# Feed-forward layer of a Perceiver kernel: weight blocks split three tiles ahead, output products four tiles behind, variances and powers of seven token tiles made in the layer before

## The chip, the cores and the metric

The kernel runs on one core of a Trainium2 chip. The metric is the device time of one launch in microseconds (us), the median of several runs. The engines are named as in the profile: PE is TensorE's matrix products, PEld its loads of the stationary operand (they overlap PE), DVE is VectorE, ACT is ScalarE, POOL is GpSimd, SP issues most of the DMAs. Every engine works through its own instructions in program order and waits on semaphores for the others.

## The reference, cut to what matters

Six layers follow each other on x, 16 sequences of 64 tokens with 512 features: 1024 tokens, which the kernel holds as 8 tiles of 128. The change touches the last two.

```python
x = x + _L1_attn_ref(_layernorm(x), ...)    # decayed attention: a scan over 64 steps, then y @ W_o.T
x = x + _L1_ffn_ref(_layernorm(x), ...)     # feed-forward

h = einsum('bsd,df->bsf', x, w1) + b1       # 512 -> 2048
h = float2fix(h, 8)                         # round to multiples of 1/256
h = pwlin_gelu_basic(h, 8, 8)               # 33-point piecewise linear GELU
out = einsum('bsf,fd->bsd', h, w2) + b2     # 2048 -> 512
return float2fix(out, 8)
```

A layernorm is (x - mean) / sqrt(variance + 1e-5) for each token.

## The kernel before

The layers run one after another. Between two of them all engines meet at a barrier, short blocks of semaphore instructions (L2376, L2378) come next, and then each engine starts on its own program of the next layer.

**The scan layer** (`decayed_attention_layer`) does 64 steps in NG = 8 groups of G = 8. Its output product of the last group, `out_proj(7)`, ends on PE after the last step; DVE then adds it to x in `add_out(7)` (L1956). Ahead of that addition DVE makes the statistics of token tiles 0 to 6 for the next layer: seven `bn_stats` (L2028) and seven `bn_aggr` (L2031), mean and variance into `mv6`. GpSimd's last work in this layer is long done by then.

**The feed-forward layer** (`feed_forward_layer`) works on NGR = 2 groups of TG = 4 token tiles (512 tokens), and in each on FT = 16 tiles of 128 hidden features: N = 32 tiles, numbered n. Its entry: DVE adds epsilon to four variances (`var6`, L2292), makes the statistics of token tile 7 (L2293, L2294) and adds epsilon to the other four (L2295); GpSimd raises each four to the power -1/2 (`rs6`, L2112). DVE normalises four tiles (`norm`, L2265), PE turns them (`turn`, L2149), ACT copies the rounded high part into `xT` (`norm_out`, L2170) and DVE makes the rest, the low part (`rest_x`, L2258). Group 1's four tiles go the same way between the tiles n = 1 and 11.

For every tile n:

- ACT copies a 128x128x4 block of w1 as the high part (`first_w`, L2175), DVE makes its low part (`rest_w`, L2270). The blocks lie in a ring of WR = 3.
- PE makes `hidden(n)` (L109): 12 products of 512 columns, high by high, high by low and low by high for four feature blocks, in one of three banks.
- ACT scales and adds the bias (L2181) and rounds (L2186), in `stage_a(n)`; DVE clamps (`round_(n)`, L2230 and L2234).
- ACT finds the knot and evaluates GELU at the two ends of the step, in `stage_b(n)` (L2196, L2199, L2201); GpSimd takes their difference (`slope(n)`, L2106).
- DVE interpolates in four instructions (`interpolate(n)`, L2245, L2248, L2250, L2252), into `hs`, a ring of HR = 4.
- PE makes `output(n)` (L2137): four fp32 products of 512 columns, which the trace shows as eight, added up over the 16 tiles of a group in four banks.

The program order is written by hand. On PE it is `hidden(n)` and then `output(n - LAG)` with LAG = 3, and after the last hidden tile the three outputs that are left. On ACT it is `first_w(n + 2)` (from n = 1), `stage_a(n + 1)`, `stage_b(n)`. On DVE it is `round_(n + 1)`, `rest_w(n + 2)` (from n = 1), `interpolate(n)`, then what belongs to single tiles: `norm` of a tile of group 1 behind n = 1, 3, 5, 7, `rest_x` behind n = 4, 6, 8, 10. When group 0 is complete, DVE takes its four banks (`sum_out`, L2282) behind `interpolate(17)` and finishes one tile (`finish`, L2288, L2289) behind each of n = 18 to 21. PE's `output(16)`, the first of group 1, waits for each bank to be taken; it stands behind `hidden(19)`. The end of the kernel is `sum_out` and `finish` of the four tiles of group 1 and their DMAs to DRAM.

The two order lines that matter are

```python
for n in range(N):                       # PE
    hidden(n)
    ...
    if n >= LAG:
        output(n - LAG)
```

Of the kernel before, what the change touches and what calls it, by code (L numbers as in the profile page):

```python
# [11 lines left out]
ALU = mybir.AluOpType  # L12
# [3 lines left out]
P = 128  # L16
B, S, D = 16, 64, 512
J, C = 512, 384
NT = B * S // P
# [10 lines left out]
LN_EPS = 1e-5  # L30
# [1554 lines left out]
def decayed_attention_layer(nc, a, e):  # L1585
# [9 lines left out]
    with ExitStack() as st:  # L1595
# [43 lines left out]

        e.open_sems()  # L1640
        with nc.Block() as block:
# [20 lines left out]
            @block.gpsimd  # L1662
            def _(pool):
                for c in range(NG):
                    ln.pool(pool, c)

# [203 lines left out]
            def _(ve):  # L1870
# [161 lines left out]
                ch.link(ins)  # L2032
                add_out(NG - 1)


def feed_forward_layer(nc, a, e):
# [13 lines left out]
    with ExitStack() as st:  # L2050
        def sbuf(name, shape, dt=F32):
            return st.enter_context(nc.sbuf_tensor(name, shape, dt))

        WR, HR, LAG = 3, 4, 3
# [9 lines left out]
        st6, mv6, var6, rs6 = e.st6, e.mv6, sbuf("var6", [P, NT]), sbuf("rs6", [P, NT])  # L2064
        xn = z
        var_sb, rs_sb, n_sb, n_mm = sem("var6s"), sem("rs6s"), sem("n_sb6"), sem("n_mm6")
# [19 lines left out]
        with nc.Block() as block:  # L2086
# [13 lines left out]
            def _(pool):  # L2100
# [8 lines left out]
                for g in range(NGR):  # L2109
                    now = slice(g * TG, (g + 1) * TG)  # L2110
                    pool.wait_ge(var_sb, BASE + g + 1)
                    nc.gpsimd.tensor_tensor(rs6[:, now], var6[:, now],  # L2112
                                            cn[:, CN_MHALF:CN_MHALF + 1].to_broadcast([P, TG]),
                                            ALU.pow).then_inc(rs_sb, 1)
# [51 lines left out]
            def _(act):  # L2166
# [45 lines left out]
                for n in range(N):  # L2212
                    if n and n + 2 < N:
                        first_w(n + 2)
# [7 lines left out]
            def _(ve):  # L2222
# [38 lines left out]
                def norm(t):  # L2261
                    ve.wait_ge(rs_sb, BASE + t // TG + 1)
# [29 lines left out]
                nc.vector.tensor_scalar(var6[:, 0:TG], mv6[:, 0:TG, 1], LN_EPS, None, ALU.add).then_inc(var_sb, 1)  # L2292
                ch.link(nc.vector.bn_stats(st6[:, NT - 1, :], x[:, NT - 1, :]))  # L2293
                ch.link(nc.vector.bn_aggr(mv6[:, NT - 1, :], st6[:, NT - 1, :]))  # L2294
                nc.vector.tensor_scalar(var6[:, TG:NT], mv6[:, TG:NT, 1], LN_EPS, None, ALU.add).then_inc(var_sb, 1)  # L2295
# [6 lines left out]
                rest_w(2)  # L2302
                ve.wait_ge(s_b, BASE + 32)
# [3 lines left out]
                for n in range(N):  # L2307
                    if n + 1 < N:
                        round_(n + 1)
                    if n and n + 2 < N:  # L2310
                        rest_w(n + 2)
# [15 lines left out]
def perceiver_kernel(nc, a, out):  # L2327

    ctx = ExitStack()
    with ctx:  # L2330
# [76 lines left out]
        env.mv6 = x[:, NT, 64:64 + NT * 2].rearrange("p (t s) -> p t s", t=NT)  # L2407
        env.out, env.xg_d, env.yg_d, env.x_d = out, xg_d, yg_d, x_d
# [66 lines left out]
```

## Time and profile before

| | us |
|---|---|
| median of 3 runs | 2140.75 |
| lowest and highest | 2139.08, 2141.41 |
| the profiled execution | 2137.46 |
| its span | 2135.7 |
| PE busy | 1910.4 (89%) |
| DVE busy | 1345.1 (63%) |
| ACT busy | 1137.0 (53%) |
| POOL busy | 124.1 (6%) |
| mean granted TensorE clock | 0.935 |

All times in the rows are microseconds from the start of the span, and durations unless a column says otherwise. The scan layer ends at about 1905, the feed-forward layer starts at 1906.6 and runs to the end: some 229 us of 2135.7. A clock of 1.00 is 2.4 GHz, of 0.50 it is 1.2 GHz. "[0.33 <-DVE ws L2270]" behind a row says that the engine was idle for 0.33 us ahead of it, until the named instruction released it; "<-issue" names no instruction that it waited for.

### The profile page before, as it was taken

The numbers are of one execution on the slowest core, as the hardware profiler recorded it, in microseconds if no ns is written. First come the engines' busy times: TensorE is split into PE (matmuls) and PEld (weight loads), VectorE is DVE, ScalarE is ACT, GpSimd is POOL, SyncE is SP. The second block draws the span as 40 slices with busy tenths as digits, with TensorE's granted clock in tenths as the row PEclk, the third lists the DMA queues.
The fourth block names the chain that finished last, engine by engine and source line by source line (L and its number), as shares of the span: only waits on it lengthen the run. The fifth ranks groups of instructions, "written<-read, shape, count | busy, mean of one in ns | idle before, by whom it ended". The sixth has DMA issues, their size and how long they took to land. (4 is left out here: it accounts for less than half of the span.)

```text
span 2135.7 us, 31829 instructions
## 1 busy us (share of the span) xinstructions
PE 1910.4 (89%) x10570; PEld 1511.8 (71%) x10570; DVE 1345.1 (63%) x2457; ACT 1137.0 (53%) x1878; POOL 124.1 (6%) x153
## 2 busy tenths in 40 slices
PE   7978875599999589999999999999977999888998
PEld 4647764599999467787878787878755676665654
DVE  4755663599999364545353636363527899986676
ACT  5753331588888254444453535454435666656654
POOL 0000001200000111000000000000000000001221
PEclk9998985799999799999999999999998788879999
DMA  7410004244431521100000000000204000020000
GB/s 259 158 55 1 0 0 202 87 175 152 187 142 54 202 75 60 35 30 34 29 34 29 34 29 34 29 34 29 79 28 147 1 1 1 1 84 1 0 20 20
DMA packets 25897, 137.47 MB, mean 64 GB/s; under 512 B 4066, under 2 KB 4194, under 8 KB 22116
## 3 DMA queue, kind: packets, MB, share of 16 engines
q1 hardware_dynamic: 19588, 116.18, 14.7%
q0 software_dynamic: 6240, 20.45, 2.8%
q8 instruction: 33, 0.54, 0.1%
q14 instruction: 36, 0.29, 0.0%
HBM read 116.17 MB, written 20.45 MB: 64 GB/s over the span
## 5 line engine op out<-in xcount | busy, mean ns | idle before, releaser
L109 PE MATMUL PS<-cT,qs 128*128 128x512 f32 x1152 | 295.5, 402 | 9.0 <-ACT pb L1406 7.0
L109 PE MATMUL PS<-pT,cN 128*128 128x512 f32 x1152 | 270.2, 392 | 1.7 <-DVE pT L1501 1.7
L109 PEld LDWEIGHTS PS<-cT,qs 128*128 128x128 f32 x1152 | 209.4, 189 | 59.8 <-issue 15.1
L109 PEld LDWEIGHTS PS<-pT,cN 128*128 128x128 f32 x1152 | 213.9, 188 | 45.5 <-DVE pT L1501 1.9
L109 PE MATMUL PS<-fw,xgT 128*128 128x384 f32 x1104 | 204.2, 340 | 3.1 <-DVE xgT L1049 3.0
L109 PEld LDWEIGHTS PS<-fw,xgT 128*128 128x128 f32 x1104 | 191.5, 189 | 8.4 <-issue 4.5
L1049 DVE TENSOR_TENSOR fw<-W,fw 128x1536 fp32r<-128x1536 f32 x92 | 159.3, 1753 | 44.7 <-ACT fw L972 44.7
L1496 DVE TENSOR_REDUCE nmax<-PS 128x1 f32<-128x512 f32 x128 | 87.7, 685 | 157.0 <-PE PS L109 156.9
L109 PE MATMUL PS<-ws,xT 128*128 128x512 f32 x672 | 180.6, 427 | 6.6 <-DVE ws L563 4.9
L109 PEld LDWEIGHTS PS<-ws,xT 128*128 128x128 f32 x672 | 137.6, 207 | 46.1 <-issue 11.3
L972 ACT ACTIVATE fw<-W 128x1536 fp32r x92 | 134.2, 1486 | 50.2 <-issue 50.2
L1401 ACT ACTIVATE qp<-PS 128x512 f32<-128x512 f32 x96 | 57.4, 598 | 189.8 <-PE PS L109 189.8
L1501 DVE TENSOR_TENSOR pT<-PS,pT 128x512 fp32r<-128x512 f32 x128 | 86.9, 684 | 52.6 <-ACT pT L1423 52.6
L2137 PE MATMUL PS<-W,hs 128*128 128x512 f32 x256 | 114.9, 593 | 2.9 <-DVE z L2282 1.7
L109 PE MATMUL PS<-xT,ws 128*128 128x512 f32 x384 | 103.0, 418 | 9.8 <-DVE ws L2270 8.4
L1423 ACT ACTIVATE pT<-PS 128x512 fp32r<-128x512 f32 x128 | 75.5, 597 | 65.6 <-PE PS L1301 65.4
L946 PE MATMUL PS<-pw,hT 128*128 128x512 f32 x414 | 101.8, 400 | 4.7 <-DVE hT L1049 4.7
L1406 ACT ACTIVATE pb<-PS,nmax 128x512 f32<-128x512 f32 x128 | 87.5, 684 | 34.4 <-DVE nmax L1496 34.3
L1713 PEld LDWEIGHTS PS<-cn,W 128*128 128x128 f32 x512 | 79.0, 228 | 36.9 <-DVE W L2025 30.3
L109 PEld LDWEIGHTS PS<-xT,ws 128*128 128x128 f32 x384 | 72.7, 191 | 38.7 <-DVE ws L2270 18.1
L1713 PE MATMUL PS<-cn,W 128*128 128x16 f32 x512 | 78.1, 287 | 21.9 <-DVE W L2025 21.7
L1524 DVE COPY qp<-PS 128x512 f32<-128x512 f32 x48 | 33.1, 691 | 100.0 <-PE PS L1338 100.0
(259 smaller groups left out, 3390.6 us busy)
## 6 DMA issues: line engine op xcount, KB each, us to landing
W<-in_fc SPq DMA_DIRECT2D x8, 3072.0 KB, 10.5
cT<-in_ctxT SPq DMA_DIRECT2D x16, 768.0 KB, 5.4
raw_pj<-in_proj SPq DMA_DIRECT2D x8, 1536.0 KB, 6.5
ct_in<-in_ctxT SPq DMA_DIRECT2D x16, 768.0 KB
cn_in<-in_ctxN SPq DMA_DIRECT2D x16, 768.0 KB
W<-in_w SPq DMA_DIRECT2D x2, 4096.0 KB, 12.9
routed_x<-zero SPq DMA_DIRECT2D x23, 256.0 KB, 5.4
xg<-routed_x POOLq DMA_DIRECT2D x23, 256.0 KB, 3.2
```

What stands on the lines that cost most here:

```text
L109: mm = nc.tensor.matmul(out, lhs(m, s), rhs(n, s), start=(opens and (s, m, n) == terms[0]), stop=((s, m, n) == terms[-1]))
L946: mm = nc.tensor.matmul(ps[7], hT[m][:, f, :], pw[n][:, f, :], start=(f == 0 and m == n), stop=(f == FK - 1 and m == 1))
L972: nc.scalar.activation(fw[0][:, :, fc_cols(c)], raw_fc_of(par, c), ACT.Copy).then_inc(fc_hi, 1)
L1049: return nc.vector.tensor_tensor(out, whole, first.bitcast(F32), ALU.subtract)
L1401: nc.scalar.activation(out, src, ACT.Copy, scale=scale).then_inc(w_sb, count)
L1406: nc.scalar.activation(pb[:, g % 2, :], ps[g % 2], ACT.Exp, bias=nmax[:, g % 4:g % 4 + 1], accum_out=rsum[:, g % 4:g % 4 + 1]).then_inc(e_ ...
L1423: nc.scalar.activation(turned(pT[0], g), ps[2 + g % 2].rearrange("p (j n) -> p j n", j=JK), ACT.Copy).then_inc(pt_hi, 1)
L1496: nc.vector.tensor_reduce(nmax[:, g % 4:g % 4 + 1], ps[g % 2], AX.X, ALU.max, negate=True).then_inc(m_dve, 1)
L1501: return nc.vector.tensor_tensor(out, whole, first.bitcast(F32), ALU.subtract)
L1524: nc.vector.tensor_copy(heads, src).then_inc(qp_dve, 1)
L1713: mm = nc.tensor.matmul(ps[6 + c % 2][:, col:col + B], rb[:, t % RB, k * P:(k + 1) * P], sel, start=True, stop=True)
L2137: mm = nc.tensor.matmul(ps[HB + t], hs[:, n % HR, t * P:(t + 1) * P], w26[:, f, :], start=(f == 0), stop=(f == FT - 1))
```

## The change

Four things are edited; nothing that is computed changes.

- The variances plus epsilon of token tiles 0 to 6 are made on DVE in the scan layer, between `bn_aggr` and `add_out(7)`, in one instruction, and GpSimd raises them to the power there, ahead of the barrier. `var6` and `rs6` move into a spare row of x, and two more semaphores carry the two hand-overs.
- In the feed-forward layer the first four `norm` are the first instructions of DVE. The statistics, the epsilon and the power of token tile 7 come later, behind `rest_w(2)`. Only `norm(7)` waits for GpSimd.
- Weight blocks are split one tile earlier: `first_w(n + 3)` and `rest_w(n + 3)` from n = 0, in the same ring of three.
- LAG is 4: PE makes `hidden(n)` and then `output(n - 4)`, and four outputs follow the last hidden tile. The ring of `hs` stays at four.

```diff
@@ scan layer, GpSimd, behind its last normalisation
+                pool.wait_ge(var_sb, BASE + 1)
+                nc.gpsimd.tensor_tensor(e.rs6[:, 0:NT - 1], e.var6[:, 0:NT - 1],
+                                        cn[:, CN_MHALF:CN_MHALF + 1].to_broadcast([P, NT - 1]), ALU.pow).then_inc(rs_sb, 1)
+                pool.wait_ge(rs_sb, BASE + 1)
@@ scan layer, DVE, its end
                 for t in range(NT - 1):
                     ins = nc.vector.bn_aggr(e.mv6[:, t, :], e.st6[:, t, :])
                 ch.link(ins)
+                nc.vector.tensor_scalar(e.var6[:, 0:NT - 1], e.mv6[:, 0:NT - 1, 1], LN_EPS, None,
+                                        ALU.add).then_inc(var_sb, 1)
                 add_out(NG - 1)
@@ feed-forward layer
-        WR, HR, LAG = 3, 4, 3
+        WR, HR, LAG = 3, 4, 4
...
@@ GpSimd
-                for g in range(NGR):
-                    now = slice(g * TG, (g + 1) * TG)
-                    pool.wait_ge(var_sb, BASE + g + 1)
-                    nc.gpsimd.tensor_tensor(rs6[:, now], var6[:, now],
-                                            cn[:, CN_MHALF:CN_MHALF + 1].to_broadcast([P, TG]),
-                                            ALU.pow).then_inc(rs_sb, 1)
+                pool.wait_ge(var_sb, BASE + 1)
+                nc.gpsimd.tensor_tensor(rs6[:, NT - 1:NT], var6[:, NT - 1:NT], cn[:, CN_MHALF:CN_MHALF + 1],
+                                        ALU.pow).then_inc(rs_sb, 1)
@@ ACT
-                    if n and n + 2 < N:
-                        first_w(n + 2)
+                    if n + WR < N:
+                        first_w(n + WR)
@@ DVE
                 def norm(t):
-                    ve.wait_ge(rs_sb, BASE + t // TG + 1)
+                    if t == NT - 1:
+                        ve.wait_ge(rs_sb, BASE + 1)
...
-                nc.vector.tensor_scalar(var6[:, 0:TG], mv6[:, 0:TG, 1], LN_EPS, None, ALU.add).then_inc(var_sb, 1)
-                ch.link(nc.vector.bn_stats(st6[:, NT - 1, :], x[:, NT - 1, :]))
-                ch.link(nc.vector.bn_aggr(mv6[:, NT - 1, :], st6[:, NT - 1, :]))
-                nc.vector.tensor_scalar(var6[:, TG:NT], mv6[:, TG:NT, 1], LN_EPS, None, ALU.add).then_inc(var_sb, 1)
                 for t in range(TG):
                     norm(t)
                 rest_w(0)
...
                 rest_w(1)
                 rest_w(2)
+                ch.link(nc.vector.bn_stats(st6[:, NT - 1, :], x[:, NT - 1, :]))
+                ch.link(nc.vector.bn_aggr(mv6[:, NT - 1, :], st6[:, NT - 1, :]))
+                nc.vector.tensor_scalar(var6[:, NT - 1:NT], mv6[:, NT - 1:NT, 1], LN_EPS, None,
+                                        ALU.add).then_inc(var_sb, 1)
...
                     if n + 1 < N:
                         round_(n + 1)
-                    if n and n + 2 < N:
-                        rest_w(n + 2)
+                    if n + WR < N:
+                        rest_w(n + WR)
                     interpolate(n)
```

The lines below are programs in order, one row for one kind of instruction, with its output and inputs; in the changed kernel the lines of the file stand some further down, so the same instruction has another number. First PE, from the start of the feed-forward layer: the turns of group 0 (z to PS), hidden tiles (ws by xT) and output tiles (hs by W). Before:

```order
L2149 MATMUL PS<-cn,z 128x128 x16
L109 MATMUL PS<-xT,ws 128x512 x48
L2137 MATMUL PS<-W,hs 128x512 x4
L109 MATMUL PS<-xT,ws 128x512 x12
L2137 MATMUL PS<-W,hs 128x512 x4
```

And in the changed kernel:

```order
L2153 MATMUL PS<-cn,z 128x128 x16
L109 MATMUL PS<-xT,ws 128x512 x60
L2141 MATMUL PS<-W,hs 128x512 x4
L109 MATMUL PS<-xT,ws 128x512 x12
L2153 MATMUL PS<-cn,z 128x128 x4
```

Five hidden tiles (60 products) now stand ahead of `output(0)`, where four stood.

Second DVE, from the last statistics of the scan layer to the weight block of tile 2. Before:

```order
L2031 BN_AGGR x<-x 128x2 x7
L1956 TENSOR_TENSOR x<-x,PS 128x512
L1641 UNCONDITIONAL_BRANCH
L2378 UNCONDITIONAL_BRANCH
L2376 UNCONDITIONAL_BRANCH
L2221 UNCONDITIONAL_BRANCH
L2292 TENSOR_SCALAR var<-x 128x4
L2293 BN_STATS x<-x 128x6
L2294 BN_AGGR x<-x 128x2
L2295 TENSOR_SCALAR var<-x 128x4
L2265 TENSOR_SCALAR z<-x,rs 128x512 x4
L2270 TENSOR_TENSOR ws<-W,ws 128x512
```

And in the changed kernel, where var6 and rs6 are parts of x:

```order
L2036 BN_AGGR x<-x 128x2 x7
L2038 TENSOR_SCALAR x<-x 128x7
L1961 TENSOR_TENSOR x<-x,PS 128x512
L1642 UNCONDITIONAL_BRANCH
L2383 UNCONDITIONAL_BRANCH
L2381 UNCONDITIONAL_BRANCH
L2225 UNCONDITIONAL_BRANCH
L2270 TENSOR_SCALAR z<-x 128x512 x4
L2275 TENSOR_TENSOR ws<-W,ws 128x512
L2262 TENSOR_TENSOR xT<-PS,xT 128x4x128 x4
L2275 TENSOR_TENSOR ws<-W,ws 128x512 x2
L2304 BN_STATS x<-x 128x6
```

The four small instructions have left the place ahead of the first normalisation (z); one of their kind stands ahead of the addition that ends the scan layer, three behind the third weight block.

Third DVE again, the first two tiles. Before, `round_(1)`, `interpolate(0)`, `round_(2)`, `rest_w(3)`, and the start of `interpolate(1)`:

```order
L2230 TENSOR_SCALAR c<-r 128x512
L2234 TENSOR_SCALAR up<-r 128x512
L2245 SCALAR_TENSOR_TENSOR y<-km,c 128x512
L2248 SCALAR_TENSOR_TENSOR y<-y,dg 128x512
L2250 SCALAR_TENSOR_TENSOR y<-g,y 128x512
L2252 SCALAR_TENSOR_TENSOR hs<-y,up 128x512
L2230 TENSOR_SCALAR c<-r 128x512
L2234 TENSOR_SCALAR up<-r 128x512
L2270 TENSOR_TENSOR ws<-W,ws 128x512
```

And in the changed kernel:

```order
L2234 TENSOR_SCALAR c<-r 128x512
L2238 TENSOR_SCALAR up<-r 128x512
L2275 TENSOR_TENSOR ws<-W,ws 128x512
L2249 SCALAR_TENSOR_TENSOR y<-km,c 128x512
L2252 SCALAR_TENSOR_TENSOR y<-y,dg 128x512
L2254 SCALAR_TENSOR_TENSOR y<-g,y 128x512
L2256 SCALAR_TENSOR_TENSOR hs<-y,up 128x512
L2234 TENSOR_SCALAR c<-r 128x512
L2238 TENSOR_SCALAR up<-r 128x512
L2275 TENSOR_TENSOR ws<-W,ws 128x512
```

`rest_w(3)` now stands ahead of `interpolate(0)`, and the block that stands behind `round_(2)` is that of tile 4.

## Rows read from the trace of the kernel before

**Rows 1.** The page's head: the span of the profiled execution.

```profile
span 2135.7 us, 31829 instructions
```

**Rows 2.** Windows: length, busy us and count of PE, PEld, DVE, ACT, POOL, clock.

```profile
1980.00:2034.00 54.00, 54.00 (x180) 33.18 (x179) 35.31 (x62) 34.31 (x54) 11.60 (x9) 1.00 0.00 0
```

**Rows 3.** Line L2270 (`rest_w`): who waited for it, us in total and times.

```profile
  PEld PS L109: 18.1, 25
```

**Rows 4.** Timeline of PEld in steady state: start, us, engine, line, operation.

```profile
1981.78 0.19 PEld L109 LDWEIGHTS PS<-xT,ws 128*128 128x128 f32 x1 [0.33 <-DVE ws L2270]
1982.12 2.47 PEld L109 LDWEIGHTS PS<-xT,ws 128*128 128x128 f32 x11 [0.16 <-issue]
...
1988.30 0.19 PEld L109 LDWEIGHTS PS<-xT,ws 128*128 128x128 f32 x1 [0.24 <-issue]
1988.73 2.48 PEld L109 LDWEIGHTS PS<-xT,ws 128*128 128x128 f32 x11 [0.24 <-issue]
...
2001.07 2.47 PEld L109 LDWEIGHTS PS<-xT,ws 128*128 128x128 f32 x11 [0.16 <-issue]
...
2007.24 2.47 PEld L109 LDWEIGHTS PS<-xT,ws 128*128 128x128 f32 x11 [0.16 <-issue]
```

**Rows 5.** Timeline of the entry into the feed-forward layer.

```profile
1904.54 0.69 DVE L1956 TENSOR_TENSOR x<-x,PS 128x512 f32<-128x512 f32 x1 [1.00 <-PE PS L1723]
...
1906.67 0.17 DVE L2292 TENSOR_SCALAR var<-x 128x4 f32<-128x4 f32 x1 [1.44 <-PEq L2376]
...
1906.92 2.09 POOL L2112 TENSOR_TENSOR rs<-var,cn 128x4 f32<-128x4 f32 x2 [96.25 <-DVE var L2292]
...
1907.97 1.92 DVE L2265 TENSOR_SCALAR z<-x,rs 128x512 f32<-128x512 f32 x4
...
1912.63 0.69 DVE L2258 TENSOR_TENSOR xT<-PS,xT 128x512 fp32r<-128x512 f32 x1 [0.16 <-ACT xT L2170]
...
1913.38 8.48 PE L109 MATMUL PS<-xT,ws 128*128 128x512 f32 x36 [1.41 <-DVE xT L2258]
```

**Rows 6.** Timeline of the first tiles, and PEld's fifth hidden tile.

```profile
1920.65 0.43 DVE L2230 TENSOR_SCALAR c<-r 128x512 f32<-128x512 f32 x1 [1.89 <-ACT r L2186]
...
1928.07 1.75 DVE L2270 TENSOR_TENSOR ws<-W,ws 128x512 fp32r<-128x512 f32 x1
...
1929.87 4.38 PE L109 MATMUL PS<-xT,ws 128*128 128x512 f32 x12 [8.01 <-DVE ws L2270]
...
1937.52 2.50 PEld L109 LDWEIGHTS PS<-xT,ws 128*128 128x128 f32 x11 [0.16 <-issue]
```

**Rows 7.** Windows of half a us, columns as in rows 2: where the clock changes.

```profile
1908.50:1909.00 0.50, 0.43 (x4) 0.43 (x4) 0.50 (x3) 0.00 (x0) 0.50 (x1) 0.92 0.94 360
...
1912.00:1912.50 0.50, 0.00 (x0) 0.00 (x0) 0.47 (x1) 0.50 (x2) 0.00 (x0) 0.67 0.15 66
...
1925.50:1926.00 0.50, 0.00 (x0) 0.00 (x0) 0.50 (x1) 0.50 (x2) 0.00 (x0) 0.99 0.00 0
...
1932.50:1933.00 0.50, 0.50 (x3) 0.36 (x3) 0.50 (x2) 0.00 (x0) 0.00 (x0) 0.68 0.00 0
```

**Rows 8.** Timeline at the group boundary: PEld's hidden tiles and DVE's `sum_out`.

```profile
2031.91 2.24 PEld L109 LDWEIGHTS PS<-xT,ws 128*128 128x128 f32 x10 [0.16 <-issue]
...
2035.62 2.48 DVE L2282 TENSOR_TENSOR z<-PS,b 128x512 f32<-128x512 f32 x4
...
2046.79 2.47 PEld L109 LDWEIGHTS PS<-xT,ws 128*128 128x128 f32 x11 [0.16 <-issue]
...
2071.93 2.47 PEld L109 LDWEIGHTS PS<-xT,ws 128*128 128x128 f32 x11 [0.16 <-issue]
```

**Rows 9.** Timeline of the tail: the last `hs`, and PE's last two output tiles.

```profile
2111.86 0.69 ACT L2181 ACTIVATE h<-PS,b1q 128x512 f32<-128x512 f32 x1 [2.74 <-PE PS L109]
...
2119.93 7.13 PE L2137 MATMUL PS<-W,hs 128*128 128x512 f32 x16 [1.24 <-DVE hs L2252]
...
2121.97 0.69 DVE L2252 SCALAR_TENSOR_TENSOR hs<-y,up 128x512 f32<-128x512 f32 x1
```

More of the change, by code:

```diff
@@ L1638, in now @@
             return slice(G * c, G * (c + 1))
+        var_sb, rs_sb = sem("var6s"), sem("rs6s")
         e.open_sems()
@@ L2063, in feed_forward_layer @@
         y = sbuf("y6", [P, 2, 512])
-        st6, mv6, var6, rs6 = e.st6, e.mv6, sbuf("var6", [P, NT]), sbuf("rs6", [P, NT])
+        st6, mv6, var6, rs6 = e.st6, e.mv6, e.var6, e.rs6
         xn = z
-        var_sb, rs_sb, n_sb, n_mm = sem("var6s"), sem("rs6s"), sem("n_sb6"), sem("n_mm6")
+        var_sb, rs_sb, n_sb, n_mm = sem("var7s"), sem("rs7s"), sem("n_sb6"), sem("n_mm6")
         s_b, b_q, dve = sem("s_b6"), sem("b_q6"), sem("dve6")
@@ L2407, in perceiver_kernel @@
         env.mv6 = x[:, NT, 64:64 + NT * 2].rearrange("p (t s) -> p t s", t=NT)
+        env.var6, env.rs6 = x[:, NT, 96:96 + NT], x[:, NT, 112:112 + NT]
         env.out, env.xg_d, env.yg_d, env.x_d = out, xg_d, yg_d, x_d
```

## The prediction, made before the changed kernel ran

> **What bounds the kernel now.** I read the page's head first: the span is 2135.7 us [rows 1], and the profiled execution took 2137.46, so 1.76 us lie around the span. The median is 2140.75, 3.29 above that execution; I work out a difference against the profiled execution and take it from the median. The change touches only the last 229 us, so the next view is the windows of the feed-forward layer. In steady state PE is busy for 54.00 of 54 us at clock 1.00 [rows 2]: it is the bound there, DVE has 35.31 us of work and ACT 34.31. From the start of products in one hidden tile to the next it takes 2007.24 - 2001.07 = 6.17 us [rows 4]: the loads of a hidden tile are 0.228 apart ((2.47 - 0.19) / 10), so its 12 products take 2.74 us, and the rest, 3.43, is the output tile. This work is the same after the change. What can move is the time in which PE stands still between 1906 and the end, in four places.
>
> The view of who waited for whom offers more than there is: PE's loads wait 18.1 us in all, 25 times, for `rest_w` [rows 3]. In steady state such a wait is 0.33 us, and the next load then follows after 0.16 (0.49 together); a tile without the wait has 0.24 and 0.24 (0.48) [rows 4]. The second load starts when the array takes the first product, and it comes at the same point either way: the wait lies under the last output product. The Trainium skill ("TensorE: Matmul & The Clock Gate", Part 2, step-by-step) says that the next tile's weights load while this tile's products run; by that rule the 18.1 us are not for sale, and the 0.49 against 0.48 agree.
>
> **The entry.** Before, DVE's first work is at 1906.67, and the first normalisation starts at 1907.97, behind the epsilon and GpSimd's power [rows 5]. After, the normalisation is DVE's first instruction: 1.30 us sooner. DVE carries the chain from there (four normalisations, a weight block, four low parts), idle only 0.16 us before the last low part [rows 5], which may go too; I take 1.30. What is moved out costs nothing in its new places, by these covers. In the scan layer one epsilon instruction (0.17, as at 1906.67) falls into the 1.00 us in which DVE waits for PE's last output product [rows 5]. GpSimd's power follows at about 1903.8 and takes 1.05 (2.09 for two of them) [rows 5]: it ends at about 1904.9, DVE's addition at 1905.23, so the barrier is not held up, with 0.3 us of cover; a power that takes 0.7 longer would cost 0.4. Token tile 7's statistics (about 1.1 us of DVE) come behind `rest_w(2)`, at about 1913.4, and the bias follows at 1915.1. ACT needs it for `stage_a(0)`, when `hidden(0)` is done: start 1913.38 - 1.30 = 1912.08, and the first product group takes some 3.1, so 1915.2. Cover 0.1; at worst a few tenths.
>
> **The clock at the entry** is the first thing I cannot read off. PE fell to half clock within 1908.50 to 1909.00 and rose within 1912.00 to 1912.50 [rows 7], after it had been idle from 1904.4 on: about 3.4 us at half clock, all under the turns of group 0, before products began at 1913.38. After the change the turns are over by about 1909.1, PE then waits until 1912.1 for DVE, and such a stretch may come later and lie on the products. Bounds: nothing, or 3.4 us at half clock on products, which loses 1.7. The nearest row is the stretch of [rows 7] itself, and I see no reason that it should end before 1912.1 again; I take half, 0.8 lost. The skill (same page, Part 1) says the monitor runs freely and doesn't restart with the work, so that the point of change shifts between runs; by that rule the loss would also differ between executions. The sum does without it.
>
> **The first tiles.** Before, PE finishes `hidden(2)` at about 1921.9 and stands idle for 8.01 us until `rest_w(3)` is done at 1929.8 [rows 6]. That instruction waits behind the whole `interpolate(0)`, which waits for GELU's table and for GpSimd. After, `rest_w(3)` stands behind `round_(1)`, 0.43 + 0.42 after 1920.65 - 1.30 [rows 6], so it is ready at 1920.9, and `hidden(3)` goes almost without a wait (0.3 us). Then PE stands before `hidden(4)`, for the block that is now in the old place of `rest_w(3)`: DVE and ACT do the same before it, shifted by 1.30. It starts at 1929.87 - 1.30 = 1928.6. So the stop stays (about 5 us in place of 8), but one more hidden tile is done ahead of it: 2.74 us gained. Here the clock comes in again: it fell at about 1926.0 and rose at about 1932.8 [rows 7], and the tile at 1929.87 took until 1937.52 where 6.17 and 0.22 for the first load would have made 1936.26 [rows 6]: 1.26 lost. A stop of 5 us may lose up to 1.7, or nothing, which is 0.44 less or 1.26 more than before; I take the same loss as before, since an idle time of 4.2 us at the entry already brought the fall [rows 7].
>
> Behind it DVE must keep up: `rest_w(4)` will take 1.75, as the block in this place does now next to GpSimd's difference, where 0.69 is usual [rows 6]. The skill ("GPSIMD Engine Reference", Key points) says that GpSimd shares its SBUF interfaces with a VectorE instruction of two SBUF inputs; by the rule the stretch is of this kind. I count `interpolate(1)` 2.9, `norm(4)` 0.54, `round_(3)` 0.85, `rest_w(5)` 0.69 from 1928.6: 1933.6, against `output(0)` ending at 1928.6 + 0.2 + 2.74 + 3.43 = 1935.0. One more stretch of 1.06 still fits.
>
> **The group boundary.** From product to product it takes 2046.79 - 2031.91 = 14.88 us for two tiles, where 12.34 are due: 2.54 lost [rows 8]. `sum_out` (2.48) starts at 2035.62, `output(16)` waits for it, and `hidden(20)` for the weight block behind it. The next four tiles take 2071.93 - 2046.79 = 25.14 for 24.68: 0.46 more, from the four `finish` on DVE. Together 3.00. After, `output(15)` stands behind `hidden(19)`, so `sum_out` must wait 3.43 us longer for it, with DVE idle; but `rest_w(20)` is done before that, and PE has `hidden(20)`, 2.74 us, while DVE takes the banks; the first is free after 0.7. Then `rest_w(21)` is due 2.74 + 3.43 = 6.17 after `output(15)` and ready at 2.48 + 0.85 + 0.69 = 4.0. DVE's tile with a `finish` is 0.43 + 0.42 + 0.69 + 4 x 0.69 + 1.12 = 5.4 us with some gaps, under 6.17, so it catches up. All 3.00 gained; at least 0.
>
> **The tail.** The last hidden tile's result is taken at 2111.86; its `hs` is ready at 2122.66, and PE stood idle for 1.24 for the one before it [rows 9]. After, four outputs (13.7 us) stand between `hidden(31)` and `output(31)`, more than the 10.8 that `hs(31)` needs. 1.24 gained. What follows, four times `sum_out` and `finish`, is unchanged.
>
> **The ring of hs** has four places, and LAG = 4 leaves none spare: `interpolate(n)` needs `output(n - 4)`. DVE comes to it behind `round_(n + 1)`, thus behind `hidden(n + 1)`, which stands behind `output(n - 4)` on PE. The wait is over before it is met.
>
> **Sum:** 1.30 + 2.74 + 3.00 + 1.24 = 8.28, less 0.8 for the clock at the entry: 7.5 us. 2137.46 - 7.5 = 2129.96 for the profiled execution, 2140.75 - 7.5 = 2133.2 for the median. With the clock at its best (0 and 1.26 back) 9.5, 2131.2; at its worst (1.7 and 0.44) 6.1, 2134.6.
>
> **Rivals.** (1) The stop at the boundary stays: DVE stands still longest there, since `sum_out` now waits for `output(15)`, and the work behind it might reach PE after all. For: DVE idles 2.5 us more. Against: 2.1 us of cover at `rest_w(21)`. Price 3.00; with the clock at its worst the gain is 3.1: 2137.6, within 0.2%. (2) Slower: DVE becomes the bound, by meeting GpSimd. In steady state GpSimd's difference runs while DVE waits for it; should the new order put `rest_w` and another two-input instruction of each tile next to it, each stretches from 0.69 to 1.75 [rows 6], and DVE's tile grows from 4.3 plus 0.2 of gaps to 6.6, past 6.17. It decides from 6.17 on, and costs 0.43 on 28 tiles, 12 us: 2145.2. Against it: `rest_w(n + 3)` takes the very slot of `rest_w(n + 2)`. (3) The load waits do cost array time: 18.1 more, 2115. [rows 4] speak against it. (4) The change does nothing at the entry, since GpSimd's power holds the barrier as long as it did the normalisation: 1.30 less, 2134.5, inside my case.
>
> **How the numbers follow.** My case 0.76 (2131.2 to 2134.6), rival 1 0.12, rival 2 0.06, rival 3 0.03, others 0.03. A median of three lies within about 1.7 of another (2139.08 to 2141.41), so the range is 2131.2 - 1.7 = 2129.5 up to 2137.5, into rival 1. A measurement tells about 0.2%, 4.3 us, from no change: faster 0.84, same 0.10, slower 0.06.
>
> **What would show it.** The first normalisation right behind the barrier, at 1906.7; a stop of about 5 us before the fifth hidden tile and none before the fourth; tiles of 6.17 with load gaps of 0.24; no wait of PE at the boundary and at the last outputs; the clock's half-rate stretches between 1909 and 1933. It would be wrong if DVE's low parts of weights came later than their tile, if tiles of 6.17 grew, or if the stop before `hidden(4)` were as long as the old one.

## The result, and the profile after the change

The changed kernel takes 2133.49 us in the median of 20 runs (2130.25 to 2138.08); the kernel before took 2140.01 in 20 runs beside it (2136.43 to 2144.98). The ratio is 0.9968, with a 95% interval of 0.996 to 0.9977: about 6.9 us faster by the ratio, 6.5 by the two medians. The prediction was 2133.2 and 7.5 us.

The profiled executions tell less at first sight: 2136.46 us with a span of 2134.6 after, against 2137.46 and 2135.7 [rows 1], only 1 us apart. The reason lies ahead of the layer. The last statistics of the scan layer are the same instruction in both kernels, and nothing ahead of them was changed; yet they start at 1898.69 before and at 1903.15 after. The first row below is of the kernel before, the others of the changed one (timeline: start, us, engine, line, operation, and in brackets what the engine waited for):

```profile
1898.69 4.25 DVE L2028 BATCH_NORM_STATS2 x<-x 128x6 f32<-128x512 f32 x7
```

```profile
1903.15 4.25 DVE L2033 BATCH_NORM_STATS2 x<-x 128x6 f32<-128x512 f32 x7
...
1908.04 0.17 DVE L2038 TENSOR_SCALAR x<-x 128x7 f32<-128x7 f32 x1
1908.29 1.49 POOL L1668 TENSOR_TENSOR x<-x,cn 128x7 f32<-128x7 f32 x1 [93.55 <-DVE x L2038]
...
1910.64 0.69 DVE L1961 TENSOR_TENSOR x<-x,PS 128x512 f32<-128x512 f32 x1 [2.42 <-PE PS L1728]
...
1912.76 1.92 DVE L2270 TENSOR_SCALAR z<-x 128x512 f32<-128x512 f32 x4 [1.44 <-PEq L2381]
```

So this execution came to the changed code 4.46 us late. In the 14 traces of this case the same instructions start anywhere from 1896.13 (e4 below, mean granted clock of the execution 0.937) to 1906.29 (e5, 0.929). And DVE waited 2.42 for the scan layer's last products instead of 1.00 [rows 5], since they ran at half clock and took 5.40 us, where the trace of before has 3.70 (the timeline of PE, before and after):

```profile
1900.73 3.70 PE L1723 MATMUL PS<-W,yT 128*128 128x512 f32 x8 [1.18 <-ACT yT L1811]
```

```profile
1905.20 5.40 PE L1728 MATMUL PS<-W,yT 128*128 128x512 f32 x8 [1.18 <-ACT yT L1816]
```

That isn't the change's either: the traces of e1 and e2 below, which have the old entry, show the same 5.40, as do all others; of 14 traces that of before alone has 3.70. Whoever compares the two spans puts these 6 us on the change. I compare the layer with itself: from the start of DVE's first instruction in it to the end of DVE's last. Before, 1906.67 [rows 5] to 2131.77; after, 1912.76 to 2130.80. The ends are these rows, before and after:

```profile
2131.08 0.69 DVE L2289 SCALAR_TENSOR_TENSOR x<-z,x 128x512 f32<-128x512 f32 x1
```

```profile
2130.11 0.69 DVE L2294 SCALAR_TENSOR_TENSOR x<-z,x 128x512 f32<-128x512 f32 x1
```

That is 225.10 against 218.04: **7.06 us shorter**, which agrees with the medians. Everything below is read on this measure, called the layer's time.

**The start after the change.** The timeline of PE, with the DVE instructions it waits for. It answers to [rows 5, 6]:

```profile
1918.36 8.46 PE L109 MATMUL PS<-xT,ws 128*128 128x512 f32 x36 [1.41 <-DVE xT L2262]
...
1926.29 0.68 DVE L2275 TENSOR_TENSOR ws<-W,ws 128x512 fp32r<-128x512 f32 x1
...
1927.03 3.01 PE L109 MATMUL PS<-xT,ws 128*128 128x512 f32 x12 [0.21 <-DVE ws L2275]
...
1931.78 0.69 DVE L2256 SCALAR_TENSOR_TENSOR hs<-y,up 128x512 f32<-128x512 f32 x1
...
1933.06 1.76 DVE L2275 TENSOR_TENSOR ws<-W,ws 128x512 fp32r<-128x512 f32 x1
...
1934.87 5.49 PE L109 MATMUL PS<-xT,ws 128*128 128x512 f32 x12 [4.83 <-DVE ws L2275]
...
1943.40 0.19 PEld L109 LDWEIGHTS PS<-xT,ws 128*128 128x128 f32 x1 [0.24 <-issue]
```

The stop of 8.01 us ahead of `hidden(3)` [rows 6] is gone (0.21 is left), and one of 4.83 stands ahead of `hidden(4)`. The windows show the clock there; column eight is the granted clock:

```profile
1933.50:1934.00 0.50, 0.00 (x0) 0.00 (x0) 0.50 (x1) 0.47 (x2) 0.50 (x1) 0.79 0.00 0
1934.00:1934.50 0.50, 0.00 (x0) 0.00 (x0) 0.50 (x1) 0.50 (x2) 0.27 (x1) 0.50 0.00 0
...
1940.50:1941.00 0.50, 0.50 (x2) 0.18 (x1) 0.47 (x2) 0.50 (x1) 0.00 (x0) 0.88 0.00 0
```

From its start `hidden(4)` needs until 1943.40 - 1934.87 = 8.53 us to the next hidden tile's load; 5.96 are due (a tile of 6.17 and 0.22 for the first load, less 0.43 from a first load to the second). So the clock takes 2.57 here, where it took 1.26 in the trace of before. By these windows it fell at 1933.8 and rose at 1940.6: 6.8 us at half clock, as long as the stretch from 1926.0 to 1932.8 in [rows 7].

**Steady state and boundary.** The window is again 54 of 54 us of PE at full clock, as [rows 2]; the timeline of PEld and DVE around the group boundary answers to [rows 4, 8]:

```profile
1984.00:2038.00 54.00, 54.00 (x179) 32.86 (x177) 34.87 (x60) 34.50 (x54) 10.32 (x8) 1.00 0.00 0
```

```profile
2031.60 0.19 PEld L109 LDWEIGHTS PS<-xT,ws 128*128 128x128 f32 x1 [0.24 <-issue]
...
2037.77 0.19 PEld L109 LDWEIGHTS PS<-xT,ws 128*128 128x128 f32 x1 [0.24 <-issue]
...
2038.40 2.48 DVE L2287 TENSOR_TENSOR z<-PS,b 128x512 f32<-128x512 f32 x4 [2.57 <-PE PS L2141]
...
2041.46 0.69 DVE L2275 TENSOR_TENSOR ws<-W,ws 128x512 fp32r<-128x512 f32 x1
...
2043.93 0.19 PEld L109 LDWEIGHTS PS<-xT,ws 128*128 128x128 f32 x1 [0.24 <-issue]
...
2050.10 0.19 PEld L109 LDWEIGHTS PS<-xT,ws 128*128 128x128 f32 x1 [0.24 <-issue]
```

Three tiles, 18.50 us, 6.17 each: nothing is lost at the boundary, though DVE now stands idle for 2.57 ahead of `sum_out`. It is close, though: each of the next four tiles, those with a `finish`, takes DVE 6.21 us (its `round_` starts at 2040.80, 2047.01, 2053.22, 2059.43 and 2065.64), a little more than PE's 6.17. Who waited for `rest_w` (line L2275) shrank from [rows 3] to

```profile
  PEld PS L109: 6.1, 3
```

and the tile still takes 6.17. Twelve us of load waits left the profile and brought nothing.

**The tail.** PE's 40 last output products come in one piece; before, the last 16 stood behind a wait of 1.24 [rows 9]:

```profile
2108.76 17.33 PE L2141 MATMUL PS<-W,hs 128*128 128x512 f32 x40
```

In the page's chain (section 4, shares of the span) the engines' row is now

```profile
PE 9%; DVE 0%; ACT 0%; issue 0%; POOL 0%; DVEq 0%
```

so the end hangs on PE's own work alone, back to the stop at the start.

**Where the 7.06 us are:** first products 5.60 us after DVE's first instruction instead of 6.71, 1.11; one more hidden tile ahead of the stop, 2.74; clock in the stop, -1.31; boundary, 3.00; tail, 1.52 (the wait of 1.24 and the loads behind it). Sum 7.06.

Two of these terms belong to the executions and not to the change. The -1.31 is one: e3 below has the old stop of 8.02 us and loses 2.6 behind it, and the changed kernel in a second trace (e12) loses 1.3 behind its stop of 4.82. The 1.11 is the other: on the way to the first products lie the turns, and they took 3.39 us in the trace of before and 3.58 in that of after, by where half clock fell. Where half clock covers the turns whole, the products start 6.99 us after DVE's first instruction with the old entry (e1, e2) and 5.69 with the new one (e6, e11, e12): 1.30. Without the clock the traces give 1.30 + 2.74 + 3.00 + 1.52 = 8.56. The medians give 6.5, and their interval reaches from 4.9 to 8.6. Whether more clock is lost in the changed kernel on the mean of many executions, one or two traces of each kernel can't tell.

### The profile page after: what moved, and what is told of

The parts are those of the page before. It is cut to its first block and busy times, and to the rows that moved or that the text cites. A ratio compares the mean times of both kernels' runs of the same rounds, so it can differ in the third digit from the quotient of the medians.

```text
span 2134.6 us, 31828 instructions
## 1 busy us (share of the span) xinstructions
PE 1920.8 (90%) x10570; PEld 1522.1 (71%) x10570; DVE 1352.5 (63%) x2457; ACT 1137.2 (53%) x1878; POOL 125.5 (6%) x153
```

## The experiments

Theory A works as the prediction does, place by place along PE's order, but it was written behind the result and knows more: in e1, e2 and e4 it says that the lag of four costs at the start, which the prediction does not. Its rival, B, is told with each run; in these three it leaves that cost out, as the prediction does. "h5" is the first load of `hidden(5)`, in us from DVE's first instruction of the layer: 36.71 before (with outputs 0 and 1 done), 30.64 after (output 0 done). The table has all runs; ratios are against the kernel before on the same chip.

| kernel | median us (runs) | ratio [95%] | layer's time | h5 |
|---|---|---|---|---|
| before | 2140.01 (20) | 1 | 225.10 | 36.71 |
| after | 2133.49 (20) | 0.9968 [0.996, 0.9977] | 218.04 | 30.64 |
| e1_weights | 2135.31 (12) | 0.9976 [0.9963, 0.9988] | 221.07 | |
| e2_lag | 2148.30 (11) | 1.0037 [1.0024, 1.0051] | 234.43 | 40.92 |
| e3_entry | 2139.63 (12) | 0.9995 [0.9984, 1.0006] | 225.43 | |
| e4_lag3 | 2132.78 (12) | 0.9965 [0.9955, 0.9974] | 218.03 | 30.67 |
| e5_lag3_then_4 | 2129.01 (4) | 0.9941 [0.992, 0.9962] | 214.60 | 30.66 |
| e6_fill_stop | 2133.39 (1) | | 217.59 | 30.19 |
| e7_four_ahead | 2129.57 (5) | 0.9945 [0.9928, 0.9961] | 216.23 | 23.28 |
| e8_four_gelu | 2129.62 (4) | 0.9941 [0.9918, 0.9963] | 216.16 | 22.72 |
| e9_two_more | 2133.75 (1) | | 218.10 | |
| e10_four_more | 2132.82 (1) | | 218.54 | 30.23 |
| e11_turns_apart | 2125.60 (4) | 0.9927 [0.991, 0.9945] | 212.43 | 25.04 |
| e12_changed_again | 2131.48 (4) | 0.9956 [0.9939, 0.9974] | 218.95 | 31.50 |

### One part at a time

**e1_weights** is the kernel before with weight blocks three ahead and nothing else (both on ACT, `first_w`, and on DVE, `rest_w`):

```diff
-                    if n and n + 2 < N:
-                        rest_w(n + 2)
+                    if n + WR < N:
+                        rest_w(n + WR)
```

> The kernel before with the weight blocks three tiles ahead alone, LAG = 3. Measured in the trace from DVE's first instruction of the feed-forward layer to its last (225.1 us before, 218.0 in the changed kernel). Theory A (four separate places): hidden(3) runs at once, and output(0), which needs only hs(0), fills the rest of the first stop; PE idles 2.5 to 3 us there in place of 8, the clock does not fall, and the fifth hidden tile starts some 6.4 us sooner. At the boundary PE still waits about 1.7 us for the banks, the last outputs still wait 1.24. About 7.7 us shorter: 217.4; median about 2132.5. Theory B (as the prediction put it, the stop before the fifth hidden tile is there at either lag and one hidden tile is gained): 2.7 at the start and 3.0 at the boundary, 219.4.

The layer took 221.07, where A had said 217.4 and B 219.4. Its order is A's: the stop stands behind `hidden(3)`. But there PE waits for `hs(0)`, and this is what followed (timeline of PE):

```profile
1934.88 5.37 PE L2137 MATMUL PS<-W,hs 128*128 128x512 f32 x8 [2.54 <-DVE hs L2252]
```

Eight output products due in 3.6 us took 5.37 after a stop of only 2.54: the granted clock was 1.00 until 1936.0 and 0.50 until 1939.4, so it fell when PE was at work again. That cost 1.7, and a stretch of half clock on the first products 1.5 more. A had taken neither; 221.07 - 3.2 = 217.9 is its number within 0.5. The 221.07 itself lies nearer to B's 219.4; it is the row, one stop of 2.54 with `output(0)` behind it, that speaks for A. Weights alone are faster (0.9976).

**e2_lag** is the kernel before with `LAG = 4` alone.

```diff
-        WR, HR, LAG = 3, 4, 3
+        WR, HR, LAG = 3, 4, 4
```

> The kernel before with LAG = 4 alone. Theory A: at the start the fifth hidden tile waits as before but output(0) now stands behind it, about 3.4 us lost; at the boundary the weight block of hidden(20) waits behind the later taking of the banks, 4.0 lost in place of 3.0; 1.24 gained at the end. 3.2 us longer: 228.3, median about 2143.2. Theory B (the lag gives the boundary and the tail by itself): 4.2 us shorter, 220.9.

It is slower, as A has it and B not, but by more than A's 228.3 (layer's time 234.43). Two rows of PE at the start:

```profile
1934.87 5.49 PE L109 MATMUL PS<-xT,ws 128*128 128x512 f32 x12 [8.02 <-DVE ws L2270]
...
1943.28 4.61 PE L109 MATMUL PS<-xT,ws 128*128 128x512 f32 x12 [2.93 <-DVE ws L2270]
```

The output tile that would have filled the time between `hidden(3)` and `hidden(4)` is now due after them, and PE stands twice, at half clock after each. At the boundary two tiles took 18.04 where 12.34 are due (2.54 were lost in before [rows 8]), since `sum_out` comes later and the weight block, two ahead, with it:

```profile
2039.02 0.19 PEld L109 LDWEIGHTS PS<-xT,ws 128*128 128x128 f32 x1 [0.32 <-DVE ws L2270]
...
2049.54 4.17 PEld L109 LDWEIGHTS PS<-xT,ws 128*128 128x128 f32 x12 [4.67 <-DVE ws L2270]
...
2057.06 0.19 PEld L109 LDWEIGHTS PS<-xT,ws 128*128 128x128 f32 x1 [0.32 <-DVE ws L2270]
```

A had left out that the boundary gets worse when the lag grows without the weights. Only the tail's wait is gone. The longer lag needs the longer lead.

**e3_entry** has only the variances and powers moved (the changed kernel with `LAG = 3` and weights two ahead).

```diff
-        WR, HR, LAG = 3, 4, 4
+        WR, HR, LAG = 3, 4, 3
...
-                    if n + WR < N:
-                        rest_w(n + WR)
+                    if n and n + 2 < N:
+                        rest_w(n + 2)
```

> The kernel before with the variances and powers moved alone (LAG = 3, weights two ahead). Theory A: the first normalisation is 1.30 us sooner, the products start 1.1 to 1.3 us sooner: 223.9, median about 2138.8. Theory B (the barrier is held up by GpSimd's power in its new place, or the half-rate clock comes to lie on the first products): no gain or up to 0.6 us longer.

The first normalisation is DVE's first instruction, and the products start 1.08 sooner. The old stop ahead of `hidden(3)` is there again:

```profile
1928.04 5.49 PE L109 MATMUL PS<-xT,ws 128*128 128x512 f32 x12 [8.02 <-DVE ws L2275]
```

The stop is as long as in the kernel before (8.01), but half clock lasted 10.2 us around it instead of 6.8, the tile behind it lost 2.6 instead of 1.3, and the layer took 225.43. So the clock loss behind one and the same stop differs by 1.3 between executions. The median cannot tell a gain of 1 us (0.9995, 0.9984 to 1.0006).

**e4_lag3** is the changed kernel with the old lag.

```diff
-        WR, HR, LAG = 3, 4, 4
+        WR, HR, LAG = 3, 4, 3
```

> The changed kernel with LAG = 3. Theory A: the sum of the two runs before it on its parts, 7.7 + 1.2 = 8.9 us shorter: 216.2, that is 1.8 us shorter than the changed kernel; what LAG = 4 gives at the boundary (1.7) and the end (1.24) is less than what it costs at the start (output(0) behind the stop before hidden(4), 2.4 us, and the clock there, 2.6 us). Theory B: LAG = 4 is worth its boundary and tail, 2.9 us or more: 220.9 or more without it.

B (220.9 or more) falls: the layer took 218.03, the same as the changed kernel. A's 216.2 missed the clock's 1.7 again. The rows show two opposite things, at the start and at the boundary:

```profile
1925.40 5.37 PE L2141 MATMUL PS<-W,hs 128*128 128x512 f32 x8 [2.55 <-DVE hs L2256]
...
2028.72 2.48 DVE L2287 TENSOR_TENSOR z<-PS,b 128x512 f32<-128x512 f32 x4
2029.56 3.67 PE L2141 MATMUL PS<-W,hs 128*128 128x512 f32 x8 [1.66 <-DVE z L2287]
```

With lag 3 PE takes `output(0)` within the time that it must stand anyway: `hidden(5)` begins at 30.67 with two outputs done, against 30.64 with one. That is an output tile, 3.4 us, for which the changed kernel has nothing in the stop: its `hs(0)` is ready at 1932.47 (the row of line L2256 above), PE is free, and the order says `hidden(4)` first. At the boundary lag 3 loses 1.9 (8.06 from product to product where 6.17 are due), in the tail 1.5. **In these two traces a lag of four costs 3.4 at the start and gives 3.4 back later.** The second 3.4 is order alone. Of the first, 2.28 is idle time of PE (4.83 against 2.55) and 1.0 is clock: 2.57 against 1.77 behind the stop, and 0.17 ahead of the first products. With the 1.3 that the same program lost in e12 it would be 2.1. The medians tell no difference (0.9965 and 0.9968). My sum had the second half and not the first; it had no place for it, since it compared with a kernel in which `output(0)` was not ready in the stop either.

### Each side apart

**e5_lag3_then_4** lets outputs lag three tiles up to `hidden(11)`, and four from `hidden(13)` on; behind `hidden(12)` comes none. It is the changed kernel otherwise.

```diff
+        SWITCH = 12
...
-                    if n >= LAG:
+                    if n < SWITCH and n >= LAG - 1:
+                        output(n - LAG + 1)
+                    elif n > SWITCH:
```

> The changed kernel with LAG = 3 up to the twelfth hidden tile and 4 from there. Measured from DVE's first instruction of the feed-forward layer to its last (218.0 us in the changed kernel and with LAG = 3 alike). Theory A (the lag costs 3.4 us at the start and gives back 3.4 at the boundary and the end, and the two don't touch each other): 218.0 - 3.4 = 214.6; median some 3.4 below the changed kernel, 2130. Theory B (the two kernels agree because something else sets 218.0): 218 again.

The layer took 214.60, to a tenth A's 218.0 - 3.4. The fair neighbour is e4, which has the same half-clock stretches: 218.03 less its 1.9 at the boundary and 1.5 in the tail is 214.6. PE waits neither at the boundary nor in the tail, and the start has e4's row again:

```profile
1935.60 5.37 PE L2142 MATMUL PS<-W,hs 128*128 128x512 f32 x8 [2.57 <-DVE hs L2259]
```

The median is 2129.01. By the ratios that is under e4 and the changed kernel, but the intervals touch (0.992 to 0.9962, against 0.9955 to 0.9974 and 0.996 to 0.9977), so it is the layer's time that carries this.

**e6_fill_stop** puts 18 products that nobody reads into a free bank ahead of `hidden(4)`, to keep PE at work in the stop.

```diff
+                    if n == 4:
+                        for k in range(18):
+                            nc.tensor.matmul(ps[7], xT[0][0][:, 0, 0:P], xT[0][0][:, k % DK, :], start=True, stop=True)
```

> The changed kernel with 18 products that nobody reads, put on PE into the stop before hidden(4), about 4.1 us of its 4.8. Theory A (the idle time brings the half-rate clock, which costs 2.6 us there): the clock stays at 1.00, hidden(4) starts at the same time and takes 2.7 in place of 5.3, 218.0 - 2.6 = 215.4. Theory B (the half rate is set by something else): half rate again, 218.0.

```profile
1929.44 4.24 PE L2161 MATMUL PS<-xT 128*128 128x512 f32 x18
...
1934.42 3.06 PE L109 MATMUL PS<-xT,ws 128*128 128x512 f32 x12 [0.74 <-DVE ws L2278]
```

The clock stays at 1.00 and `hidden(4)` takes 3.06 in place of 5.49; from it to `hidden(5)` it is 5.90, not 8.53, 2.63 back. So the loss in the stop is the clock's and not a load's or a buffer's. It is one execution, but the others bear it out: in twelve of the 14 traces PE stands 2.5 us or more somewhere between `hidden(2)` and the second turn of the next group, and half clock comes each time; in e6 and e11 it does not stand so long, and there is none. The layer's time shows only 0.45 of it (217.59), since half clock lay on the first products in this execution (10.73 us for three tiles where 8.67 are due): 218.04 - 2.63 + 2.06 = 217.5.

**e9_two_more** and **e10_four_more** measure the cover at the boundary, by additions on DVE right behind `sum_out` whose result nobody reads, two and four of them.

```diff
+                        for _ in range(2):
+                            ch.link(nc.vector.tensor_tensor(y[:, 0, :], b2[:, :], b2[:, :], ALU.add))
```

> The changed kernel with two more additions of 128x512 on DVE behind the four sum_out of the group boundary (1.45 us) that nobody reads. Theory A (the low part of the block for tile 21 is ready 1.8 us before PE asks for it, so the boundary has that much cover): nothing moves on PE, no wait at the boundary. Theory B (the boundary's cover is used up, as the first rival of the prediction had it): about 1.4 us longer from there on.

> The same with four such additions (2.9 us). Theory A: past the cover of 1.8 us; PE waits 1.1 to 1.3 us before hidden(21), the rest is caught up. Theory B: 2.9 us.

With two (1.41 us) the loads of the hidden tiles are still 6.17 apart:

```profile
2038.05 1.41 DVE L2326 TENSOR_TENSOR y<-b 128x512 f32<-128x512 f32 x2
...
2041.19 0.19 PEld L109 LDWEIGHTS PS<-xT,ws 128*128 128x128 f32 x1 [0.24 <-issue]
...
2047.35 0.19 PEld L109 LDWEIGHTS PS<-xT,ws 128*128 128x128 f32 x1 [0.24 <-issue]
```

With four (2.86 us) PE waits:

```profile
2036.30 2.86 DVE L2326 TENSOR_TENSOR y<-b 128x512 f32<-128x512 f32 x4
...
2040.61 3.04 PE L109 MATMUL PS<-xT,ws 128*128 128x512 f32 x12 [0.58 <-DVE ws L2275]
```

The layer was 0.50 longer than in the changed kernel with a start 0.41 shorter (h5), so 2.86 us cost 0.9 (A had 1.1 to 1.3): the cover is 2.0 us. The prediction worked out 2.1. Both are single executions; the rows carry this, not the times.

### Does one more tile ahead give one more gain?

**e7_four_ahead** splits weight blocks four tiles ahead on ACT and DVE.

```diff
-                    if n + WR < N:
-                        rest_w(n + WR)
+                    if n == 0:
+                        rest_w(3)
+                    if n + 4 < N:
+                        rest_w(n + 4)
```

> The changed kernel with the weight blocks one tile further ahead, in the same ring of three: the copy for tile n + 4 behind stage_a(n + 1) on ACT, the low part behind round_(n + 1) on DVE. Theory A (the stop before hidden(4) is there only because its block stands behind interpolate(0)): PE runs through hidden(4), waits 0.3 us for output(0), the clock stays at 1.00, hidden(5) starts 23.8 us after DVE's first instruction in place of 30.6: 218.0 - 6.8 = 211.2; median about 2127. Theory B (the stop is the pace of ACT and DVE at the start and only moves on to the next tiles): 215 or more.

The first half of A holds: no stop ahead of `hidden(4)`, 0.38 ahead of `output(0)`, full clock, and h5 at 23.28 where A said 23.8.

```profile
1923.85 5.74 PE L109 MATMUL PS<-xT,ws 128*128 128x512 f32 x24 [0.21 <-DVE ws L2277]
...
1929.96 3.67 PE L2141 MATMUL PS<-W,hs 128*128 128x512 f32 x8 [0.38 <-DVE hs L2258]
...
1952.83 0.63 PE L2153 MATMUL PS<-cn,z 128*128 128x128 f32 x4 [3.38 <-DVE xT L2264]
1953.29 5.30 PE L2141 MATMUL PS<-W,hs 128*128 128x512 f32 x8
```

The third row is why the layer took 216.23 and not 211.2: at the second turn of the next group PE waits 3.38 for DVE to have taken the first turn out of the one bank they share, and the clock falls again (5.30 for 3.6). DVE is still behind from the start; the wait that ended at `hidden(4)`, 22.1 after DVE's first instruction, now ends 21 us later, at 43.1, and is smaller. B's mechanism, in part.

**e8_four_gelu** adds to e7 a GELU of one column, ahead of `stage_a(0)`, so that the table is there early.

```diff
+                nc.scalar.activation(junk[:, :], cn[:, CN_K0:CN_K0 + 1], ACT.Gelu)
```

> The kernel with the blocks four ahead, and one GELU of a single column on ACT ahead of stage_a(0), so that the table is loaded (1.28 us) while ACT waits for hidden(0). Theory A: the first hs is 1.28 us sooner, but PE's wait for it was only 0.3: 210.9. Theory B (the table load stands in the chain that holds PE there): 1.28 less than with the blocks alone.

```profile
1950.65 1.09 PE L2154 MATMUL PS<-cn,z 128*128 128x128 f32 x4 [2.99 <-DVE xT L2266]
```

h5 came 0.56 sooner, and the second turn 1.26 sooner (41.81 after DVE's first instruction, 43.07 in e7). That is the table's 1.28, as B has it: it did stand in the chain that holds PE. But half clock lasted 6.8 us behind this stop and 3.4 in e7, and from the turn to the next hidden tile it took 6.41 instead of 5.20. So the layer took 216.16, and what the table gave the clock of this execution took. The medians tell no difference (2129.62 and 2129.57).

**e11_turns_apart** is e8 with the turns of the next group three tiles apart instead of two.

```diff
-        NORM_AT = [1 + 2 * t for t in range(TG)]
+        NORM_AT = [1 + 3 * t for t in range(TG)]
```

> The kernel with the blocks four ahead and the early GELU, and the normalisations of group 1 behind tiles 1, 4, 7, 10 in place of 1, 3, 5, 7 (their turns and low parts follow at the same distances). Theory A (with the stop gone DVE is behind, and PE waits 3 us at the second turn because the one bank of the turns is not read yet): with one tile more between two turns most of that wait goes: 216.2 - 3 or more, 212 to 213 us from DVE's first instruction to its last; median about 2127. Theory B (DVE's lag is the pace, wherever PE meets it): PE waits the same time at another place, 216.

No engine's wait is left on PE from 1920 on but this 0.21:

```profile
1915.13 10.56 PE L109 MATMUL PS<-xT,ws 128*128 128x512 f32 x36 [1.41 <-DVE xT L2266]
...
1925.91 5.74 PE L109 MATMUL PS<-xT,ws 128*128 128x512 f32 x24 [0.21 <-DVE ws L2279]
```

The layer took 212.43, as A said (212 to 213), and in this are 2.1 us of half clock on the first products (10.56 for 36, where the changed kernel took 8.46). The median, 2125.6, is the lowest of all: ratio 0.9927 to the kernel before, 0.991 to 0.9945. Its interval overlaps those of e5, e7 and e8, but the same program as the changed kernel took 2131.48 beside it on the same chip (e12), and the slowest of its four runs is below the fastest of e12's. It is the version to keep.

### The same kernel once more

**e12_changed_again** is the changed kernel, unchanged, to see what of its trace is the execution's.

> The changed kernel once more, for a second trace. Theory A (what differs between executions is where the half-rate stretches fall): the same instructions wait the same times, and the feed-forward layer differs from 218.0 us only by stretches on the first product groups, by up to 2.1 us. Theory B: other waits differ too.

```profile
1924.07 3.02 PE L109 MATMUL PS<-xT,ws 128*128 128x512 f32 x12 [0.21 <-DVE ws L2275]
...
1931.91 4.36 PE L109 MATMUL PS<-xT,ws 128*128 128x512 f32 x12 [4.82 <-DVE ws L2275]
```

The waits repeat to a hundredth (0.21, 4.82 for 0.21, 4.83). The clock does not: the tile behind the stop lost 1.3, as before the change, in place of 2.6, and the first products lost 2.1 in place of nothing. Together 218.95 in place of 218.04. Half clock on the first products came in e1, e2, e6, e11 and e12 (1.5 us with the old entry, 2.1 with the new), and not in before, after, e3, e4, e5, e7 to e10. It comes with the old entry (two traces of three) and with the new (three of eleven), so nothing here lays it on the change.

## Why the prediction was right, step by step

- **Entry**: 1.30 forecast, 1.11 in the trace of after (1.08 in e3), and 1.30 where the turns ran at like clock (6.99 against 5.69, above). The normalisation did start right behind the barrier. The power took 1.49, not 1.05 (seven columns in one instruction), and ended at 1909.78, ahead of the end of DVE's addition at 1911.33. With the wait of 1.00 in the trace of before it would have ended about 0.1 us behind the addition, not 0.3 ahead; but the addition is late in every trace with the new entry (a wait of 2.42, at half clock), and the cover is 1.5. I had read it from the one trace that was the exception.
- **Clock at the entry**: the mechanism was wrong here. I took 0.8, half of what the stretch of [rows 7] would cost if it came later and lay on the products. It did not move so: in the eleven traces with the new entry half clock either lasted 3.4 us and was over at the latest 4.0 after DVE's first instruction, before the products at 5.4 to 5.6, or it lasted 10.2 us, until 10.2, and took 2.1. So the loss is 0 or 2.1, the bound of 1.7 was too low, and the long stretch comes with the kernel before as well (1.5 in e1 and e2). No run shows that the change brings any of it. That the 0.8 moved the sum towards the measured medians was luck. The Trainium skill ("TensorE: Matmul & The Clock Gate", Part 1) says that the monitor runs freely, and the sentence in the prediction that the loss would then differ between executions is what the traces show.
- **One more hidden tile ahead of the stop**: 2.74, as forecast, and the stop was 4.83 for "about 5".
- **Clock in the stop**: the term that was mis-sized. I kept the 1.26 of before and bounded it by 1.7. It was 2.57 in the trace of after and 1.3 in e12, and e6 shows that it is all clock. I had the bound from the 3.4 us stretch of the entry, and yet the stretch at this very place was 6.8 us long in [rows 7], from 1926.0 to 1932.8. It began 4.1 us into the stop. Of a stop of 5 us that leaves 0.9, so up to 5.9 us of half clock lie on products and cost up to 2.9; that was the bound to take. The term isn't the change's alone either: e3 lost 2.6 behind the old stop.
- **Boundary**: 3.00 of 3.00, with a cover of 2.0 for 2.1. What I had not parted: 1.1 of it comes from the weights, 1.9 from the lag (e4). And one step failed without harm: I had DVE at 5.4 us with some gaps for a tile with a `finish`, so that it would catch up. It took 6.21, past PE's 6.17, since the first instruction of `finish` took 1.52 in place of 0.43; over four tiles that is 0.16, and the cover bore it.
- **Tail**: 1.24 forecast, 1.52 measured, since the first loads behind a wait are not hidden either.
- **Load waits**: worth nothing, right. They fell from 18.1 to 6.1 us and the tile stayed 6.17. Rival 3 with its 2115 falls, and with it the reading that a wait in the profile is a time to be had.
- **The other rivals**: no stop at the boundary (1), tiles of 6.17 (2; but DVE's four tiles with a `finish` passed its mark of 6.17 by 0.04 each, and nothing waited), and an entry that does give 1.1 (4).

The total, 7.5 forecast against 6.5 in the medians and 7.06 in the layer's time, rests on errors that partly cancel in this trace: entry -0.2, entry clock +0.8, stop clock -1.3, tail +0.3. The places and their order were right; that the sum came so near is in part luck of the clock. What the working did not see at all is the stop's idle time that the lag of four leaves at the start, 2.3 us and up to 3.4 with the clock. It did not spoil the sum, because the sum was made place by place against the kernel before; it would have spoiled the advice, since e5's layer is 3.4 us shorter and e11's median 5.9 under the same program as the changed kernel beside it.

## What to carry to other kernels

A lag or a lead that suits steady state need not suit the start: at the start take what is ready first, and change over later. When one stop of an in-order engine is taken away, look for the next buffer that the late engine still holds (here one turn bank, 21 us on) and move that too. Of a stop, count the clock behind it as well, with a range from several executions; and where the clock's stretches in unchanged code shift a kernel by some us, compare the changed stretch with itself.

## What the runs showed of the hardware

- The granted clock fell behind a stop as short as 2.54 us, and 0.7 to 1.2 us after PE was at work again (e1: 1.00 until 1936.0, work from 1934.88; 0.7 in e4, 0.9 in e5, 1.2 in e7; e4 and e5 show the same 5.37 for eight products). Behind the 1.66 us at the boundary and the 1.24 in the tail of the kernel before it stayed at 1.00.
- Behind a stop of 4.8 us the clock took 1.3 to 2.6 us beside the stop's own length, in the same program, and behind one of 8.0 us as well (before, e3). Half clock lasted 6.8 us there in the traces of before and after, 3.4 in e12 and 10.2 in e3.
- The same kernel lost 0 or 2.1 us of clock on the first products of the layer, from one execution to another.
- Next to GpSimd's difference DVE's two-input instructions took 1.65 to 1.78 where 0.69 is usual, and the one-input `z<-z` took 1.52 for 0.43 (timeline of the changed kernel, POOL and DVE):

```profile
2044.63 1.45 POOL L2113 TENSOR_TENSOR dg<-g 128x512 f32<-128x512 f32 x1 [4.88 <-ACT g L2205]
2044.85 1.52 DVE L2293 TENSOR_SCALAR z<-z 128x512 f32<-128x512 f32 x1
```
